# A router's matmuls laid out anew: token sums as weights on column quarters, one matmul that adds and turns the parts, one that spreads all coefficients

## What is computed

```
def _L0_ffn_ref(x, w12, b12, w3, b3):
    x1, x2 = split(einsum('bsk,mk->bsm', x, w12) + b12)
    return einsum('bsm,nm->bsn', silu(x1) * x2, w3) + b3

def _L1_ffn_ref(x, W_org, lora_down, lora_up, lora_keys, Wq):
    base = einsum('bsi,oi->bso', x, W_org)
    q = einsum('bi,ki->bk', x.mean(axis=1), Wq)             # K = 128
    scores = einsum('bk,ek->be', q, lora_keys) / sqrt(K)    # E = 8
    coeffs = softmax(scores, axis=-1)
    h = einsum('bsi,eir->bser', x, lora_down)               # R = 64
    delta = einsum('be,bser,ero->bso', coeffs, h, lora_up)
    return base + delta

x = x + _L0_ffn_ref(_L0_cond_ref(x, L0_cond_weights, itok), ...)
x = x + _L1_ffn_ref(_L1_cond_ref(x, itok, L1_cond_W, lora_A, lora_B), ...)
```

## Time and profile before

| | us |
|---|---|
| median of three runs | 1003.94 |
| lowest, highest | 1003.42, 1004.28 |
| the profiled execution | 1004.58 |
| its span | 1002.9 |
| TensorE busy in it | 992.4 |
| VectorE busy | 742.5 |
| ScalarE busy | 391.4 |
| GpSimd busy | 33.9 |

### The profile page before, as it was taken

How to read it: one execution, slowest core, us unless ns; L and a number is a source line. 1 busy time by engine, 2 the same in 40 slices (tenths; PEclk the granted TensorE clock), 3 DMA queues, 4 the chain that set the end, 5 groups by cost and what they waited for, 6 DMA issues and landing times.

```text
span 1002.9 us, 12344 instructions
## 1 busy us (share of the span) xinstructions
PE 992.4 (99%) x4776; PEld 820.0 (82%) x4776; DVE 742.5 (74%) x574; ACT 391.4 (39%) x349; POOL 33.9 (3%) x55
## 2 busy tenths in 40 slices
PE   8999999999999999999999999999999999999997
PEld 6888888888887888888898888888888888888886
DVE  2877877998866889675446888789985859877641
ACT  6563563443344333331055544543433532423110
POOL 1600000000000000000100000000000000000011
PEclk9999999999999999999999999999999999999999
DMA  9022035025014001324311211521330230031012
GB/s 348 9 85 106 1 142 193 21 93 182 1 42 143 25 1 63 149 103 170 125 43 42 84 42 38 215 85 32 118 145 2 84 127 0 1 106 42 1 63 105
DMA packets 22985, 84.68 MB, mean 84 GB/s; under 512 B 2690, under 2 KB 6802, under 8 KB 17042
## 3 DMA queue, kind: packets, MB, share of 16 engines
q1 hardware_dynamic: 20450, 75.24, 20.8%
q0 software_dynamic: 2400, 8.41, 2.2%
q10 hardware_dynamic: 80, 0.26, 0.1%
HBM read 75.51 MB, written 8.39 MB: 84 GB/s over the span
## 4 chain that ended last, share of the span: by engine, by line
PE 98%; issue 1%; DMA 0%; DVEq 0%; DVE 0%; POOLq 0%; POOL 0%; SPq 0%
PE banks L638 31%; PE banks L639 31%; PE banks L640 31%; PE banks L734 3%; PE banks L699 2%; PE banks L717 1%; DMA cond_sb<-cond_t_in 0%; PE banks L746 0%; PE banks L760 0%; DVE r L1000 0%; DVEq L454 0%; POOLq L1137 0%; POOL out_t L621 0%; DVEq L457 0%; SPq L462 0%
## 5 line engine op out<-in xcount | busy, mean ns | idle before, releaser
L638 PE MATMUL banks<-s_hi,t_hi 128*128 128x512 f32 x1360 | 531.5, 391 | 0.0
L639 PE MATMUL banks<-s_lo,t_hi 128*128 128x512 f32 x1360 | 529.4, 389 | 0.0
L640 PE MATMUL banks<-s_hi,t_lo 128*128 128x512 f32 x1360 | 529.1, 389 | 0.0
L638 PEld LDWEIGHTS banks<-s_hi,t_hi 128*128 128x128 f32 x1360 | 255.2, 188 | 56.3 <-issue 3.6
L640 PEld LDWEIGHTS banks<-s_hi,t_lo 128*128 128x128 f32 x1360 | 255.3, 188 | 53.5
L639 PEld LDWEIGHTS banks<-s_lo,t_hi 128*128 128x128 f32 x1360 | 255.3, 188 | 52.3
L1000 DVE TENSOR_TENSOR r<-banks,r 128x1024 f32<-128x1024 f32 x92 | 111.5, 1219 | 100.3 <-PE banks L640 95.7
L902 DVE TENSOR_TENSOR t_lo<-w,t_hi 128x1024 fp32r<-128x1024 f32 x132 | 156.5, 1218 | 7.0 <-ACT t_hi L832 7.0
L813 ACT CAST s_hi<-st 128x2048 fp32r<-128x2048 f32 x40 | 76.5, 1913 | 197.7 <-PE banks L640 145.0
L832 ACT CAST t_hi<-w 128x1024 fp32r<-128x1024 f32 x132 | 133.3, 1048 | 50.4 <-PE banks L640 50.4
L813 ACT CAST s_hi<-r 128x2048 fp32r<-128x2048 f32 x34 | 65.0, 1913 | 203.3 <-PE banks L640 178.3
(11 more groups left out here) (63 smaller groups left out, 358.2 us busy)
## 6 DMA issues: line engine op xcount, KB each, us to landing
w<-w_up_in SPq DMA_DIRECT2D x16, 1024.0 KB, 4.8
w<-w_base_in SPq DMA_DIRECT2D x10, 1024.0 KB, 4.8
w<-w_down_in SPq DMA_DIRECT2D x8, 1024.0 KB, 5.2
r<-x_t_in SPq DMA_DIRECT2D x8, 1024.0 KB, 6.2
w<-w_lin_in SPq DMA_DIRECT2D x8, 1024.0 KB, 5.4
out_t<-r POOLq DMA_DIRECT2D x16, 512.0 KB, 3.2
we<-w_expin_in SPq DMA_DIRECT2D x10, 512.0 KB, 4.6
st<-x_pairs_in SPq DMA_DIRECT2D x8, 512.0 KB, 7.2
```

What stands on the lines that cost most here:

```text
L638: pe.matmul(out, w_hi, x_hi, start=start, stop=False, skip_group_check=True)
L639: pe.matmul(out, w_hi, x_lo, start=False, stop=False, skip_group_check=True)
L640: return pe.matmul(out, w_lo, x_hi, start=False, stop=stop, skip_group_check=True)
```

## The change

The q product is turned round. The token sums are now the weights and Wq moves: `y_sum` is widened from 16 to 32 columns, of which the upper 16 are zeroed once by GpSimd, and matmul k writes its 32 by 128 result to partition quarter k mod 4 of `router`. So each quarter holds the sum of two of the eight parts, with sequences on partitions. VectorE copies the 128 by 128 parts to `q_parts` (a piece of `xr`). A new matmul after group 0 of product 4 has them as weights, and as moving operand `same`, a 128 by 48 matrix with ones where partition and column agree modulo 32 and 16. It adds the four quarters and turns them, and gives q three times over in 48 columns. The copy to `q_sb` comes after VectorE's `s_split` and first `t_split` beside product 4; the copy of the parts has its old place.

Scores, maximum, exponential and reciprocal then run on 48 rows, three copies of the 16. Two multiplies on VectorE write 48 by 64 coefficients, each row's on its own diagonal: rows 0 to 31 for the even experts, 32 to 47 for the odd ones. One matmul with the 48 by 128 matrix `spread` as weights, ones that GpSimd writes for each half, gives all 64 columns of coefficients that four matmuls gave before. `coef` now is a piece of `xr` too.

```diff
+        q_parts = xr[:, 0, 0:P]
+        coef = xr[:, 0, P:P + KE * BH].rearrange("p (k b) -> p k b", k=KE)
+        coef_rows = xr[0:3 * BH, 1, 0:KE * BH].rearrange("q (k b) -> q k b", k=KE)
+        spread = xr[0:3 * BH, 1, P:2 * P]
...
-            pool.memset(ident[:, :], 0.0).then_inc(consts_made, 1)
+            pool.memset(same[:, :], 0.0).then_inc(consts_made, 1)
+            pool.memset(y_sum[:, :, :], 0.0).then_inc(y_cleared, 1)
...
-            pool.affine_select(out=ident[:, :], in_=ident[:, :], compare_op=ALU.not_equal, fill=1.0, base=0,
-                               pattern=[[-1, BH]], channel_multiplier=1).then_inc(consts_made, 1)
+            for c in range(4):
+                pool.wait_ge(consts_made, 4 + c)
+                pool.affine_select(out=same[:, :], in_=same[:, :], compare_op=ALU.not_equal, fill=1.0, base=-32 * c,
+                                   pattern=[[0, 3], [-1, BH]], channel_multiplier=1).then_inc(consts_made, 1)
...
+                pool.wait_ge(group_done, group_end(phase_of(h, "lin", 6)))
+                pool.memset(spread, 0.0).then_inc(spread_made, 1)
+                pool.wait_ge(spread_made, 3 * h + 1)
+                pool.memset(xr[0:BH, 1, P:P + S], 1.0).then_inc(spread_made, 1)
+                pool.memset(xr[2 * BH:3 * BH, 1, P + S:2 * P], 1.0).then_inc(spread_made, 1)
...
                     for k in range(K):
-                        last = pe.matmul(router[:, 0:BH], wq_sb[:, k * P:(k + 1) * P], y_sum[:, k, :],
-                                         start=(k == 0), stop=(k == K - 1))
-                    last.then_inc(q_full, 1)
+                        rows = slice(32 * (k % 4), 32 * (k % 4 + 1))
+                        last = pe.matmul(router[rows, 0:KEY], y_sum[:, k, :], wq_sb[:, k * KEY:(k + 1) * KEY],
+                                         start=(k < 4), stop=(k >= 4), skip_group_check=True)
+                    last.then_inc(parts_full, 1)
+                if (i, g) == (4, 0):
+                    pe.wait_ge(parts_copied, h + 1)
+                    pe.wait_ge(consts_made, 8)
+                    pe.matmul(router[:, P:P + 3 * BH], q_parts, same[:, :], start=True, stop=True).then_inc(q_full, 1)
                 if (i, g) == (4, 1):
                     pe.wait_ge(q_copied, h + 1)
                     pe.wait_ge(small_loaded, 48)
-                    pe.matmul(router[0:BH, 32:32 + E], q_sb[:, :], keys_sb[:, :],
+                    pe.matmul(router[0:3 * BH, 2 * P:2 * P + E], q_sb[:, :], keys_sb[:, :],
                               start=True, stop=True).then_inc(scores_full, 1)
                 if (i, g) == (5, 1):
                     wait_taken(pe, n - 1, 3)
-                    pe.wait_ge(rows_done, h + 1)
-                    pe.wait_ge(consts_made, 5)
-                    for k in range(KE):
-                        rows = coef_rows[:, 2 * k:2 * k + 2, :].rearrange("b e r -> b (e r)")
-                        last = pe.matmul(coef_bank[:, k * BH:(k + 1) * BH], rows, ident[:, :],
-                                         start=True, stop=True)
-                    last.then_inc(coef_full, 1)
+                    pe.wait_ge(rows_done, 2 * (h + 1))
+                    pe.wait_ge(spread_made, 3 * (h + 1))
+                    pe.matmul(coef_bank[:, 0:KE * BH], spread, coef_rows.rearrange("q k b -> q (k b)"),
+                              start=True, stop=True).then_inc(coef_full, 1)
...
+            def copy_parts(h):
+                dve.wait_ge(parts_full, h + 1)
+                dve.tensor_copy(q_parts, router[:, 0:KEY]).then_inc(parts_copied, 1)
...
-                dve.tensor_scalar(coef_rows, sexp[:, :].unsqueeze(2).to_broadcast([BH, E, ER]),
-                                  sinv[:, :], None, ALU.mult).then_inc(rows_done, 1)
+                for odd, rows in enumerate((slice(0, 2 * BH), slice(2 * BH, 3 * BH))):
+                    n_rows = rows.stop - rows.start
+                    dve.scalar_tensor_tensor(
+                        out=coef_rows[rows, :, :], in0=same[rows, 0:BH].unsqueeze(1).to_broadcast([n_rows, KE, BH]),
+                        scalar=sinv[rows, :],
+                        in1=sexp[rows, :].rearrange("q (k o) -> q k o", o=2)[:, :, odd:odd + 1].to_broadcast(
+                            [n_rows, KE, BH]), op0=ALU.mult, op1=ALU.mult).then_inc(rows_done, 1)
...
                 if kind == "exp" and i == 4:
-                    copy_q(h)
+                    copy_parts(h)
...
                 if n < LAST:
                     t_split(n + 1, 0)
+                if kind == "exp" and i == 4:
+                    copy_q(h)
```

More of the change, by code:

```diff
@@ L285, in build @@
         half_mask = sb("half_mask", [P, 4])
[L286 to L292, removed]
+        same = sb("same", [P, 3 * BH])
+        y_sum = sb("y_sum", [P, K, 2 * BH])
+        q_sb = sb("q_sb", [P, 3 * BH])
+        smax, sbias = sb("smax", [3 * BH, 1]), sb("sbias", [3 * BH, 1])
+        ssum, sinv = sb("ssum", [3 * BH, 1]), sb("sinv", [3 * BH, 1])
+        sexp = sb("sexp", [3 * BH, E])
         banks = ctx.enter_context(nc.psum_tensor("banks", [P, 8, TN], F32))
@@ L298, in build @@
         wq_sb = cond_sb[:, :, :].rearrange("p n s -> p (n s)")
-        coef_rows = xr[0:BH, :, :].rearrange("b t (e r) -> b (t e) r", r=ER)
+        q_parts = xr[:, 0, 0:P]
+        coef = xr[:, 0, P:P + KE * BH].rearrange("p (k b) -> p k b", k=KE)
+        coef_rows = xr[0:3 * BH, 1, 0:KE * BH].rearrange("q (k b) -> q k b", k=KE)
+        spread = xr[0:3 * BH, 1, P:2 * P]
         lora_b_sb = r[:, 8, :].rearrange("p (t m) -> p t m", t=TILES)
@@ L330, in build @@
         y_summed = sem("y_summed")
+        y_cleared = sem("y_cleared")
+        parts_full, parts_copied = sem("parts_full"), sem("parts_copied")
+        spread_made = sem("spread_made")
         q_full, q_copied = sem("q_full"), sem("q_copied")
@@ L892, in scalar_engine @@
                     act.wait_ge(bias_done, h + 1)
-                    act.activation(sexp[:, :], router[0:BH, 32:32 + E], ACT.Exp, bias=sbias[:, :],
+                    act.activation(sexp[:, :], router[0:3 * BH, 2 * P:2 * P + E], ACT.Exp, bias=sbias[:, :],
                                    scale=SCORE_SCALE, accum_out=ssum[:, :]).then_inc(exp_done, 1)
@@ L1054, in sum_y @@
                 wait_block(dve, s, b)
+                dve.wait_ge(y_cleared, 1)
                 t, m = b // 2, b % 2
@@ L1058, in sum_y @@
                                   AX_X, ALU.add).then_inc(y_summed, 1)
+            def copy_parts(h):
+                dve.wait_ge(parts_full, h + 1)
+                dve.tensor_copy(q_parts, router[:, 0:KEY]).then_inc(parts_copied, 1)
             def copy_q(h):
                 dve.wait_ge(q_full, h + 1)
-                dve.tensor_copy(q_sb[:, :], router[:, 0:BH]).then_inc(q_copied, 1)
+                dve.tensor_copy(q_sb[:, :], router[:, P:P + 3 * BH]).then_inc(q_copied, 1)
             def largest(h):
                 dve.wait_ge(scores_full, h + 1)
-                dve.reduce_max(smax[:, :], router[0:BH, 32:32 + E], AX_X).then_inc(max_done, 1)
+                dve.reduce_max(smax[:, :], router[0:3 * BH, 2 * P:2 * P + E], AX_X).then_inc(max_done, 1)
                 dve.wait_ge(max_done, h + 1)
```

## The result

The changed kernel takes 1000.96 us (median of 11 runs, 999.71 to 1001.62) against 1003.11 for the kernel before in the same comparison: a ratio of 0.9976, 95% interval 0.9967 to 0.9984, so 1.6 to 3.3 us less. The forecast was 1001.3 in a range of 1000.3 to 1002.7. It was counted from 1003.94, the median of three runs of before; the eleven runs of this comparison put before at 1003.11. Taken from there, the sum of -2.66 gives 1000.45, and the measured 1000.96 is 0.5 above it.

A forecast was written before the change was run, and what follows sets the result against it. TensorE's stream was taken to bound the kernel. Per half, -1.80 + 0.78 + 0.32 + 0.03 - 1.19 + 0.53 = -1.33 us, twice -2.66, giving a median of 1001.3 us from 1003.94, range 1000.3 to 1002.7.

The forecast's parts named there:

- What bounds the kernel: TensorE, busy 992.4 of 1002.9 us: time taken from its stream is saved, an added wait costs its full length.
- What is removed: On TensorE, per half: eight q matmuls, 1.80 us, and four coefficient matmuls, 1.19 us.
- The parts, 0.78: The 16 q-product instructions on column quarters, four side by side, add 0.78 us a half.
- the gap: Weight loads ahead of the quarters idle 0.35 us; without this the parts would cost 0.55 us.
- The turn, 0.32: The matmul that adds and turns the quarters adds 0.32 us a half, bounds 0.1 to 0.52.
- Scores and coefficients: Scores with 48 weight columns: +0.03 on 0.34 us a half; one coefficient matmul: 0.53 in place of 1.19.
- The sum: All insertion terms on TensorE together: -1.33 us a half, -2.66 in all, if no new wait is exposed.
- The new waits: TensorE waiting for VectorE's copies: covered, with 1.7 us to spare at the turn and 1.0 at the scores.
- GpSimd: Its added memsets and three selects of 0.19 us each cost nothing, unless the first memset took over 7 us.
- B: Rival: quarters do not overlap, parts cost 2.1 us in place of 0.78; 0.0 gained a half, 1003.9; chance 0.05.
- C: Rival: partial TensorE wait of 0.7 us a half for VectorE's copy of q; 1002.7; chance 0.08.
- D: Rival: VectorE's copy of q 3.51 us late, TensorE waits 2.5 a half; slower, 1006.3; chance 0.05.

The follow-up runs named there:

- experiment 5: Changed kernel with VectorE's copy of q one step later, behind product 4's first add: 1003.92 us; in a second run, copy ahead of the splits: 1000.40 us.
- experiment 4: Changed kernel with all eight parts written to one partition quarter, the other three left as they are (q not the reference's): 1002.48 us in one execution.
- experiment 6: Changed kernel with scores and coefficient matmuls widened to the full 128 by 128 form, softmax on 128 rows: 998.98 us, ratio to before 0.9960.

## Why the prediction was right, point by point

- **What bounds the kernel.** This was right. The stretch of main matmuls moved by what the insertions cost, also where a wait was put in (experiment 5).
- **What is removed.** 1.80 and 1.19 a half; both profiles of before repeat them within 0.01.
- **The parts, 0.78.** This was right within 0.01 in every profile that spreads them over four quarters. Pricing them by a count within a longer group of the same form was sound. The quarters run side by side (experiment 4), and the gap is there.
- **The turn, 0.32.** This is the term that was most mis-sized, by 0.09: it measured 0.23. The step at fault was to give its two instructions the pace of a row of sixteen, 0.106 each: the next main matmul follows 0.14 after the first of them (409.54 - 409.40), not 0.21. The hold-up of the second main matmul behind them was there as reckoned (409.86 - 409.54 = 0.32).
- **Scores and coefficients.** They measured 0.39 for 0.37, and 0.57 for 0.53, both inside their bounds. The prediction put 0.01 of the 0.53 on the 48 more moving columns. The columns are not what was missing: on the whole array the same 64 columns cost one beat (experiment 6).
- **The sum.** The forecast was 1.33 a half. The four insertions of the first half give 3.33 - 1.97 = 1.36, 2.72 for both, and the stretch 2.65. The beats behind an insertion are slower than the regular one, and they account for the rest as far as starts given to 0.01 can tell. From 406.85 to 409.18 and from 409.86 to 412.17 are ten beats each, 0.11 us more together than twenty of 0.2267. Before, the 22 beats from 410.06 to 415.09 were 0.04 more than their due. That is some 0.07 a half that the change loses again, which no term of the sum had. So that 2.66 met 2.65 so closely is partly luck: a turn that was too dear made up for scores, coefficients and slow beats that were too cheap.
- **The new waits.** The copy of the parts ran at once, s_lo was unmoved, and the spare time was 0.96 us at the scores for 1.0 forecast and 1.94 at the turn for 1.7. Two small multiplies took 0.58 where one took 0.475, with 2.2 us to spare behind them.
- **GpSimd.** It was right that its work is free, though its selects took much longer than the 0.19 that the prediction had given them (below).
- **The rivals.** B's price was right (2.07 for 2.1), its condition false. C and D, a copy of q that comes too late, did not happen either. Their price of a microsecond for a microsecond is what experiment 5 shows: a wait of 1.5 a half, made by one step more in VectorE's queue, cost 3.06 us.
- **The median.** It is 2.15 less than before in the first comparison, with the interval of 1.6 to 3.3 around the 2.65 of the trace. The forecast of 1001.3 lay 0.3 above the measured 1000.96 because two differences pull against each other: the gain was 0.5 smaller in the medians than the sum, and the median of before 0.8 lower than the three runs that the forecast started from. The start of the program varies by 2.2 us over the ten profiles, nearly as much as the change is worth, and the median of a few runs carries that.

## What to carry to other kernels

Where one engine's stream is the time, price a small piece of work by the starts around it, start to start against the regular beat, and price a new form by the part of a longer group of the same form; here the removed work and the parts held to 0.01 us, and the worst term, a lone pair priced by the pace of a row of sixteen, was 0.09 off. Small matmuls on column quarters pay because four run side by side, and they must pay for a change of form on the way in and out. So pad the lone ones to the form of their neighbours (0.23 us each here, in place of 0.39 and 0.57), and use quarters where several follow in a row; eight were enough here, and fewer were not run. Give every new copy between engines a place with time to spare: one step later in VectorE's queue cost 1.5 us a time and the whole gain.

## What the runs showed of the hardware that was not expected

A matmul of two instructions in the form of its neighbours cost one beat, 0.23 us, with 8, 16, 48, 64 or 128 moving columns.

GpSimd's selects on the mask, 0.19 us in the earlier trace rows, came out longer where VectorE was subtracting two operands of 1024 elements at the time. In the profile of after VectorE's two subtractions run from 14.96 to 17.32:

```profile
14.96 2.36 DVE L919 TENSOR_TENSOR t_lo<-w,t_hi 128x1024 fp32r<-128x1024 f32 x2 [5.11 <-ACT t_hi L849]
```

```profile
15.55 0.68 POOL L607 TENSOR_SCALAR_AFFINE_SELECT mask<-mask 128x8 f32<-128x8 f32 x1
16.30 1.07 POOL L610 TENSOR_SCALAR_AFFINE_SELECT mask<-mask 128x8 f32<-128x8 f32 x1
17.51 1.38 POOL L614 TENSOR_SCALAR_AFFINE_SELECT same<-same 128x48 f32<-128x48 f32 x4
```

When the changed kernel ran again, VectorE began later. The selects on the mask were all but over by then, and now the selects on `same` were the ones that it overlapped:

```profile
15.87 2.39 DVE L919 TENSOR_TENSOR t_lo<-w,t_hi 128x1024 fp32r<-128x1024 f32 x2 [6.05 <-ACT t_hi L849]
```

```profile
15.51 0.20 POOL L607 TENSOR_SCALAR_AFFINE_SELECT mask<-mask 128x8 f32<-128x8 f32 x1
15.78 0.19 POOL L610 TENSOR_SCALAR_AFFINE_SELECT mask<-mask 128x8 f32<-128x8 f32 x1
16.12 2.99 POOL L614 TENSOR_SCALAR_AFFINE_SELECT same<-same 128x48 f32<-128x48 f32 x4
```

The same instructions take 0.20 or 0.68, 0.19 or 1.07, and 1.38 or 2.99 us, and VectorE's own take 2.36 and 2.39. The ends tell more than the lengths. VectorE's row is two subtractions, which in the first case end at 16.19 and 17.32, and the two selects on the mask end at 16.23 and 17.37. In the second case they end at 17.10 and 18.25, and the first two selects on `same`, taken singly, at 17.19 and 18.35. So a select that starts while such a subtraction runs ends just behind it, within 0.1 us. All eight profiles of kernels with the selects on `same` show the one or the other case; in the two of before the selects were over ahead of VectorE's start. GpSimd has time for it here; where it doesn't, its times beside a busy VectorE have to be taken from rows of such a stretch.
